# Mixture-of-experts stage of a fused Flamingo block: tiles fixed per expert, split weights kept, rows scattered to the output

## The reference

```python
x = x + tanh(g_xattn[0]) * L0_attention(layernorm(x), ctx)      # 32 heads, 8 KV heads
x = x + tanh(g_ffn[0])   * L0_blockdiagonal_ffn(layernorm(x))
x = x + tanh(g_xattn[1]) * L1_group_attention(layernorm(x), ctx)  # "x3" after this line
xf = layernorm(x).reshape(1024, 512)
selected = argmax(softmax(xf @ gate_w.T + gate_b))              # one of 8 experts per token
y[n] = xf[n] @ expert_w[selected[n]].T + expert_b[selected[n]]
x = x + tanh(g_ffn[1]) * y
```

## Time and profile before

| | us |
|---|---|
| median of 3 runs (840.06 to 843.03) | 842.01 |
| the profiled execution | 839.19 |
| its span, first to last instruction | 837.4 |
| busy in the span: PE / DVE / ACT / POOL | 767.1 / 484.6 / 490.6 / 344.4 |
| mean granted TensorE clock, as a share of full speed | 0.959 |

### The profile page before, as it was taken

How to read it: one execution, slowest core, us unless ns; L and a number is a source line. 1 busy time by engine, 2 the same in 40 slices (tenths; PEclk the granted TensorE clock), 3 DMA queues, 4 the chain that set the end, 5 groups by cost and what they waited for, 6 DMA issues and landing times. The chain is left out here.

```text
span 837.4 us, 13956 instructions
## 1 busy us (share of the span) xinstructions
PE 767.1 (92%) x3914; PEld 604.0 (72%) x3914; DVE 484.6 (58%) x889; ACT 490.6 (59%) x1836; POOL 344.4 (41%) x647
## 2 busy tenths in 40 slices
PE   5999988999999999999999999999999795778990
PEld 3888867888888887888887888888876242445760
DVE  4775304565655655556565655655666467646773
ACT  5543237667676675766766676676663566324760
POOL 0330024453443543444353453443322467135884
PEclk9999989999999999999999999999999799867995
DMA  9545631021021021012012003000200659513436
GB/s 306 183 122 154 188 102 64 14 76 64 13 77 63 14 76 64 13 50 88 13 32 94 25 13 113 25 13 14 101 2 10 204 179 411 196 76 117 146 127 213
DMA packets 46216, 80.68 MB, mean 96 GB/s; under 512 B 5192, under 2 KB 25672, under 8 KB 42704
## 3 DMA queue, kind: packets, MB, share of 16 engines
q1 hardware_dynamic: 43536, 71.66, 25.1%
q0 software_dynamic: 2624, 8.39, 3.0%
HBM read 55.40 MB, written 24.64 MB: 96 GB/s over the span
## 5 line engine op out<-in xcount | busy, mean ns | idle before, releaser
L557 ACT ACTIVATE p_sb<-p_sb,nmax 128x128 f32<-128x128 f32 x256 | 99.7, 391 | 132.5 <-DVE nmax L721 132.5
L649 POOL TENSOR_TENSOR v_lo<-v_raw,v_hi 128x128 fp32r<-128x128 f32 x64 | 29.7, 464 | 259.0 <-ACT v_hi L595 259.0
L744 DVE TENSOR_TENSOR pT_lo<-banks,pT_hi 128x512 fp32r<-128x512 f32 x64 | 44.3, 692 | 49.9 <-ACT pT_hi L570 49.9
L786 PEld LDWEIGHTS banks<-kT,qT_sb 128*128 128x128 f32 x512 | 67.4, 192 | 7.2 <-ACT qT_sb L565 1.8
L786 PE MATMUL banks<-kT,qT_sb 128*128 128x128 f32 x512 | 68.2, 277 | 1.4 <-ACT qT_sb L565 1.4
L654 POOL TENSOR_TENSOR p_sb<-p_sb,rsum 128x512 f32<-128x512 f32 x64 | 66.7, 1041 | 5.6 <-DVE rsum L740 5.6
L602 ACT ACTIVATE q_junk<-banks 128x128 f32<-128x128 f32 x256 | 66.2, 272 | 3.4 <-PE banks L798 3.4
L712 DVE TENSOR_TENSOR oT_lo<-banks,oT_hi 128x512 fp32r<-128x512 f32 x64 | 44.1, 689 | 36.2 <-ACT oT_hi L552 36.1
L393 PE MATMUL banks<-w_hi,ctx_hi 128*128 128x512 f32 x128 | 53.8, 420 | 8.7 <-DVE ctx_lo L324 8.6
L750 DVE SCALAR_TENSOR_TENSOR x_sb<-banks,tgates,x_sb 128x512 f32<-128x512 f32 x64 | 48.1, 751 | 19.2 <-PE banks L828 19.2
L552 ACT ACTIVATE oT_hi<-banks 128x512 fp32r<-128x512 f32 x64 | 38.1, 595 | 35.5 <-PE banks L839 31.4
(11 more groups left out here) (262 smaller groups left out, 2174.0 us busy)
## 6 DMA issues: line engine op xcount, KB each, us to landing
w_raw<-in_wq_l SPq DMA_DIRECT2D x8, 1024.0 KB, 5.6
w_raw<-in_wo_l SPq DMA_DIRECT2D x8, 1024.0 KB, 4.8
exp_w<-in_exp_w_l SPq DMA_DIRECT2D x8, 1024.0 KB, 13.5
kT_scr<-kT_st SPq DMA_DIRECT2D x16, 256.0 KB, 2.3
v_scr<-v_st SPq DMA_DIRECT2D x16, 256.0 KB, 2.3
sorted_x<-ctx_nat SPq DMA_DIRECT2D x1, 3840.0 KB, 11.9
hid<-sorted_x SPq DMA_DIRECT2D x15, 256.0 KB, 2.7
sorted_y<-ctx_nat SPq DMA_DIRECT2D x15, 256.0 KB, 2.0
```

Source lines behind the costliest of these rows:

```text
L557: last = act.activation(p_sb[:, b % 2, h * P:(h + 1) * P], p_sb[:, b % 2, h * P:(h + 1) * P], ACT.Exp, bias=nmax[:, b % 2, h:h + 1], accum ...
L786: last = pe.matmul(s_ps[:, h * P:(h + 1) * P], qT_sb[:, b % 2, h * P:(h + 1) * P], kT[:, b * P:(b + 1) * P], start=True, stop=True)
```

## The change

- The end of the block and the barrier between `middle` and `experts` are gone; both stages share one block. POOL clears the semaphores of `attention` inside `middle`, behind its fourth scatter. `keep_clock` is gone.
- The raw rows of x3 are scattered, with reciprocal root, shift and token number in 4 more columns (`ROW` = 516), to a region of 1024 rows per expert. A position no longer depends on the counts of the other experts, so the work is done in two halves of 4 blocks (`choose`, `position`, `scatter`). ACT normalises a row tile after it is loaded.
- The gate weights are centred (each column's mean subtracted) so that logits can be taken from raw rows; they are multiplied by the reciprocal root afterwards.
- Tiles 0 to 7 are the first 128 rows of each expert in a fixed `ORDER`; tiles 8 to 14 are found at run time (`list_tiles`). The weights are split once for each expert and kept, in 128 KB of each partition. DVE makes `lo` parts 0 to 2, POOL part 3 (of the first expert POOL makes all). Tiles 8 to 14 split no weights; PE and POOL read the expert number by `value_load`.
- POOL scales all biases by `tanh(g_ffn[1])` once and adds the expert's bias to the raw rows of each tile. DVE adds the product. POOL stores each tile by an indirect DMA straight to the output; rows that hold no token are out of bounds and are skipped. `sorted_y`, the gather and the last pass are gone.
- The regions are filled from one constant row during `attention` (8 DMAs of 2.1 MB). The gate's constants are loaded there too. The expert weights are loaded in the order 6, 7, then (after `y_done`) 4, 5, 0, 1, 2, 3, then the biases (2 MB).
- The tile loop is unrolled. Rows are loaded into 6 buffers, results have 3 banks.

```diff
@@ attention, SP @@
                 kT_half(1)
+                fill(g)
+            def fill(e):
+                sp.dma_start(d.sorted_x[e].rearrange("(k p) n -> p k n", p=P),
+                             s.empty[:, :].unsqueeze(1).to_broadcast([P, B, ROW])).then_inc(s.filled, 16)
...
+            fill(0)
             loads(1)
@@ middle @@
             for jt in range(KT):
                 scatter(0, jt)
+            nc.clear_and_free_semaphores(s.stage_sems)
+            pool.memset(s.recycled_flag[:, :], 0.0).then_inc(s.recycled, 1)
             scale_ctx(range(2))
...
+            for kt in range(KT):
+                pe.matmul(sm_ps[:, 320:320 + E], s.ones[:, :], s.gate_w[:, kt, :], start=(kt == 0), stop=(kt == KT - 1))
             pe.matmul(sm_ps[:, 0:B], s.group_mean[:, :], s.zmv[:, :, 0], start=True, stop=True).then_inc(gmean_done, 1)
@@ middle, SP @@
-            for e in (0, 1, 2, 3, 6, 7):
-                sp.dma_start(s.exp_w[:, e, :, :], d.exp_w[e]).then_inc(s.exp_ld, 16)
+            for e in (6, 7):
+                sp.dma_start(s.exp_w[:, e, :, :], d.exp_w[e]).then_inc(s.exp_ld[e // 2], 16)
             sp.wait_ge(y_done, B)
-            for e in (4, 5):
-                sp.dma_start(s.exp_w[:, e, :, :], d.exp_w[e]).then_inc(s.exp_ld, 16)
+            for e in (4, 5, 0, 1, 2, 3):
+                sp.dma_start(s.exp_w[:, e, :, :], d.exp_w[e]).then_inc(s.exp_ld[e // 2], 16)
+            sp.wait_ge(res_done, B)
+            sp.dma_start(s.exp_b[:, :, :], d.exp_b).then_inc(s.exp_b_ld, 16)
@@ experts, SP @@
+            sp.wait_ge(scattered, 16 * B)
+            for t in range(TILES):
+                slot = t % SLOTS
+                if t >= SLOTS:
+                    sp.wait_ge(stored[slot], 16 * (t // SLOTS))
...
+                sp.dma_start(xs[:, slot, :], rows).then_inc(xs_ld[slot], 16)
@@ experts, ACT @@
+            for b in BY_POOL:
+                act.activation(s.z[:, b, :], s.z[:, b, :], ACT.Identity, scale=s.a_col[:, b:b + 1]).then_inc(scaled_z, 1)
+            split_w(0)
+            copy_x3T(0)
...
+            copy_x3T(3)
+            seed(0)
...
+            seed(1)
+            split_w(1)
+            run([(split_x, 1), (normalise, 2), (split_next_w, 2)])
@@ experts, POOL @@
+            split_w(0, (0, 1))
+            rstd(0)
+            split_w(0, (2, 3))
+            rstd(1)
...
+            scatter(0)
+            pool.wait_ge(s.exp_b_ld, 16)
+            scatter(1)
+            pool.tensor_scalar(s.exp_b[:, :, :], s.exp_b[:, :, :], s.tgates[:, 3:4], None, ALU.mult).then_inc(bias_scaled, 1)
+            def add_bias(t):
...
+                pool.tensor_tensor(xs[:, slot, 0:D], xs[:, slot, 0:D], s.exp_b[:, e, :], ALU.add).then_inc(biased, 1)
+            def store(t):
+                pool.wait_ge(res_done, t + 1)
+                pool.indirect_dma_start(out=d.out_rows, in_=xs[:, slot, 0:D], in_offset=None,
+                                        out_offset=IndirectOffsetOnAxis(ap=xs[:, slot, TOKEN:TOKEN + 1].bitcast(I32), axis=0),
+                                        bounds_check=T - 1, oob_is_err=False).then_inc(stored[slot], 16)
+            run([(split_next_w, 1), (add_bias, 0), (store, -1)])
@@ experts, DVE @@
...
+            choose(0)
...
+            half_var(1)
+            position(0)
+            shift(1)
+            choose(1)
+            position(1)
+            run([(split_x, 1), (add_y, -1), (split_next_w, 1)])
@@ experts, PE @@
+            for b in range(B):
+                transpose_x3(b)
+                if b:
+                    gates(b - 1)
+            gates(B - 1)
...
+            ranks(0)
+            ranks(1)
...
+            run([(transpose_tile, 1), (multiply, 0)])
```

More of the change, by code:

```diff
@@ L42 @@
 EPS = 1e-5
[L43 to L46, removed]
+EXTRA = B - 1
+TILES = E + EXTRA
+ROW = D + 4
+RSTD, SHIFT, TOKEN = D, D + 1, D + 2
+ORDER = (6, 7, 4, 5, 0, 1, 2, 3)
+SLOTS = 6
+NOWHERE = 1e9
+GATE_LOADS = 8
+ARENA, SIDE = 144 * 1024, 28 * 1024
 QTOK = 2 * P
@@ L1304, in experts @@
         logit, top = m.sb("logit", [P, B, E]), m.sb("top", [P, B])
         cand, first = m.sb("cand", [P, B, E]), m.sb("first", [P, B])
[L1306 to L1309, removed]
+        hot, hot_sum = m.sb("hot", [P, B, E]), m.sb("hot_sum", [P, 2, E])
@@ L1372, in experts @@
-        stage = ExitStack()
-        block = stage.enter_context(nc.Block())
+        fuller, tiles = m.sb("fuller", [P, E, EXTRA]), m.sb("tiles", [P, E])
+        below, end = m.sb("below", [P, E, E]), m.sb("end", [P, E])
+        past, begin = m.sb("past", [P, EXTRA, E]), m.sb("begin", [P, EXTRA])
+        tile_e, tile_row = m.sb("tile_e", [P, EXTRA]), m.sb("tile_row", [P, EXTRA])
+        tile_i, row_i = m.sb("tile_i", [P, EXTRA], I32), m.sb("row_i", [P, EXTRA], I32)
+        x3T = s.xn
+        xs, xn, xsT_hi, xsT_lo = s.xs, s.xn, s.xsT_hi, s.xsT_lo
@@ new lines, in experts, with static_expert, run @@
+        BY_POOL = (4, 5)
+        LO_POOL = (3,)
+        LO_DVE = tuple(kt for kt in range(KT) if kt not in LO_POOL)
+        def static_expert(t):
+            return ORDER[t] if t < E else None
+        def run(stages):
+            last = max(-ahead for _, ahead in stages)
+            first = max(ahead for _, ahead in stages)
+            for i in range(-first, TILES + last):
+                for stage, ahead in stages:
+                    if 0 <= i + ahead < TILES:
+                        stage(i + ahead)
@@ L1401, in _ @@
+            for i in range(SLOTS):
+                sp.wait_ge(stored[i], 16 * len(range(i, TILES, SLOTS)))
         @block.scalar
@@ L1581, in split_x, with update, stats @@
-            def split_x(t, slot, r):
+            over = lambda ap, n=HB: ap.unsqueeze(1).to_broadcast([P, n, E])
+            def update(b):
+                dve.wait_ge(s.res_done, b + 1)
+                dve.scalar_tensor_tensor(out=xrow[:, b, 0:D], in0=s.z[:, b, :], scalar=s.a_col[:, b:b + 1],
+                                         in1=s.x[:, b, :], op0=ALU.mult, op1=ALU.add).then_inc(x3_done, 1)
+            def stats(b):
+                if b in BY_POOL:
+                    dve.wait_ge(x3_pool, BY_POOL.index(b) + 1)
+                else:
+                    dve.wait_ge(x3_done, b + 1 - sum(q < b for q in BY_POOL))
+                dve.bn_stats(s.bn[:, b, :], xrow[:, b, 0:D]).then_inc(bn_done, 1)
@@ new lines, in _ @@
+            dve.wait_ge(s.a_done, 1)
+            dve.wait_ge(s.centred, B)
+            update(0)
+            update(1)
+            stats(0)
+            update(2)
+            stats(1)
+            aggregate(0)
+            update(3)
+            stats(2)
+            aggregate(1)
+            stats(3)
+            aggregate(2)
+            aggregate(3)
+            half_var(0)
+            stats(4)
+            update(6)
+            aggregate(4)
+            stats(5)
+            shift(0)
@@ new lines, in gates @@
+            def gates(b):
+                pe.wait_ge(x3T_copied, b + 1)
+                for kt in range(KT):
+                    last = pe.matmul(logit_ps[b // HB][:, b % HB * E:(b % HB + 1) * E], x3T[:, b % 2, kt * P:(kt + 1) * P],
+                                     s.gate_c[:, kt, :], start=(kt == 0), stop=(kt == KT - 1))
+                last.then_inc(logit_done, 1)
+            pe.wait_ge(s.recycled, 1)
+            pe.wait_ge(s.gate_centred, 1)
+            pe.wait_ge(s.row_done, B)
```

608 lines of the change are left out of this document (288 added, 320 removed).

## The result

The changed kernel takes 846.61 us (median of 6 runs, 842.44 to 849.72) beside 841.84 for the kernel before: a ratio of 1.0055, 95% interval 1.0031 to 1.0080. In a second set of runs it was 841.25 beside 839.35, 1.0023 (1.0003 to 1.0043). The forecast was 826.0, with a range of 813 to 837 and a chance of 0.05 for slower. It was wrong.

A forecast was written before the change was run, and what follows sets the result against it. The prediction took a chain of waits as the bound: front 49.8 us, loop 54.6, tail 20.9. Terms -16.6 - 2.4 + 1.0 + 1.9 = -16.1 took the span from 837.4 to 821.3, the median to 826.0; range 813 to 837.

The forecast's parts named there:

- The tail: From the last matmul to the end: 4.3 us instead of 20.9, saving 16.6 us.
- The front: From `a_col` to the first product: gates from 716.5 at the lower clock, first product at 759.5, saving 2.4 us.
- Rival one: The front runs at the full clock, 2.4 GHz: 10 us more off, 816 us; chance 0.22.
- The drain in the middle: POOL's semaphore clearing in `middle` brings a drain that delays the scatters there: 1.0 us taken, up to 2.4.
- Rival two: POOL's indirect store in the tile loop takes 2.5 us to issue: 14 us more, 840 us; chance 0.12.
- The loop: Tile loop: POOL bounds tiles up to 7 at 4.3 us each; 1.9 us longer overall, from 3.5 shorter to 6 longer.
- The scaling of the biases: On POOL between the last scatter and the first product: 6.2 us, hidden, costing nothing.
- The last seven tiles: End of the tile loop, no weight splits: PE sets the pace at 3.3 us a tile, 1.8 us less in all.
- What hides the rest: Fills in SP's queue during attention: 6.5 us each, with 21.5 us until the load behind is used, so no cost.
- Rival three: Fills in SP's queue hold up attention's loads, from 18 us a fill; at 26 us, 48 us more, 874; chance 0.05.

The follow-up runs named there:

- e11: Changed kernel with fills half a group earlier, bias scaling and splits moved, attention's loop written out, seven idle matmuls ahead of the gates: 806.65 us, ratio 0.9603 to before.
- e8_one_column: Changed kernel with POOL's bias add cut to one of its 512 columns: 829.84 us, ratio 0.9877 to the kernel before.
- e1: Changed kernel with each 2 MB fill issued half a group earlier: 832.3 us, ratio 0.9930 to the kernel before.
- e6: Changed kernel with fills half a group earlier, bias scaling on ACT, tile list and most weight splits ahead of the first tile: 819.31 us, ratio 0.9761 to before.
- e3: Changed kernel with the bias scaling on ACT as eight instructions, not one on POOL: 837.82 us, ratio 0.9992 to the kernel before.
- e4: e3 with the tile list and most weight splits moved ahead of the tile loop, none on POOL from tile 1 on: 833.41 us, ratio 0.9947 to before.

## Why the prediction was wrong, by its own steps

*The tail: right.* It gave 4.3 us from the last product to the end; it is 5.4, and 15.5 us were saved of 16.6.

*The front: right, on the careful side.* Gates were to begin at 716.5 on before's time scale, with the clock at 0.50 throughout; they began at 732.81, which less the 16.6 us by which `a_col` is later in the first profile is 716.2, and the clock was 0.50 in every window of 4 us from 728 to 776. First product: 45.7 us after `a_col`, against 47.4 forecast and 49.9 before. Rival one, the front at full clock, did not happen, and `e11` shows that even a warmed clock does not outlast the gates.

*The drain in the middle: nothing* in the second profile, 1.0 forecast.

*Rival two, a dear store:* it did not happen. POOL's store took 1.90 us for the first tile, 1.26 where DVE's splits are beside it and 0.98 in the last seven, where 1.9 was the point from which it would decide.

*The loop, "POOL is the new bound, at 4.3": this step failed.* Tiles 2 to 7 took 29.0 us (first products at 787.46 and, of tile 8, at 816.45), 4.8 each, and tile 0 alone 8.5 (774.27 to 782.77). What bound them was neither POOL nor DVE alone but both by turns. I added up each engine's busy time, DVE 3.3 us, POOL 4.3, and took the longer sum. Where two engines need one port, what they do with it has to be added: DVE's splits 1.9 and POOL's split and addition 2.6 make 4.5, and DVE's other 1.4 lie beside that only where the order allows. That is an estimate. What the trace shows is that of the seven groups of three splits four took 1.88 us and three were held, for 3.4, 3.8 and 2.5 us (the table under `e8_one_column`). The clue was there, two POOL operations of 3.05 us beside DVE's, where they take 2.5 alone; I booked it as POOL being slower and did not ask what DVE lost. The scaling of the biases, "costs nothing" at 6.2 us, took 10.65 and reached into the loop, where it and POOL's next four operations held DVE's cast. The term came to +8.5 to +10 instead of +1.9. The last seven tiles ran at 3.2, as forecast.

*"What hides the rest", the fills at nothing: this step failed, and it was the larger one.* I asked which data stands behind a fill in SP's queue and found 21.5 us of slack, which is true: ACT never waited for a DMA at the line that was L578. What stood behind it was not data. At a branch back, ACT's instructions come through the same DMA engines, and the fill was issued 6 us ahead of it. The price is 12.8 us by the run that adds nothing else. Rival three named the place and the right victim, attention, by another mechanism and with a threshold of 18 us a fill, which the fills, at 8.8 us each and not 6.5, stayed well under; so its chance of 0.05 was no cover. In the trace of before both halves could be seen: ACT's 2.12 us of "issue" at 315.96, just at the branch, and SP's burst of loads beside it. I had not looked for idle time inside attention, since the change put no instruction there.

The Trainium skill, "Runtime: NRT & Kernel Launch", section "Instruction fetch mechanics", says that a taken branch whose target is not in the pages at hand forces a fetch of the target's page by DMA before the engine can go on. The runs agree, with 2.1 us at a quiet moment; that the wait grows to 5.9 to 6.3 us behind a fill and two loads is what they add.

With the terms at their measured size, the sum is -15.5 - 4.2 + 12 + 9 = +1.3 us; the two medians are +4.8 and +1.9. What is left of the first, 3.5 us, stays open; the two intervals overlap, and how often the stall in the middle comes was not followed further.

## What to carry to other kernels

A large transfer put into a quiet stretch is not free because the next load has slack: look where the engines' loops branch back, and keep the DMA engines empty there, or write the loop out. When work is shared out between DVE and POOL, first mark every operation of DVE that has two SBUF inputs or copies within SBUF; count the large ones and POOL's as one queue, so put their sum, not the longer of the two, against PE. And take two profiles before a stall is blamed on the change.

## What the runs showed of the hardware that I had not expected

- A branch back costs ACT 2.0 to 2.1 us with little traffic in the kernel before (2.5 to 2.8 in `e1` and `e6`) and 5.9 to 6.3 with a 2 MB fill and two 1 MB loads under way; straight code shows no stall beside the same traffic. PE's clock falls to 0.50 behind the longer stall at the first branch.
- A DVE cast of 7 columns, 0.16 us alone, took 5.60, until the last of five POOL operations without a gap was over. Without the scaling beside it in `e3` it took 0.16. Three small operations with two SBUF inputs, just ahead of it, were held for 0.25 us or not at all. POOL pays too: its indirect DMA took 1.90 us instead of 0.97 where it met a group of three splits (785.90, beside the group at 785.00), and in `e4` up to 1.50.
- POOL's one scaling of 128x4096 took 10.65 us; ACT did the same in 4.99, as eight instructions of 128x512.
- With PE busy for 4.00 of 4.00 us with short matmuls in each window from 736 to 752, the granted clock stayed at 0.50 in the changed kernel's front. In `e11` it fell from 1.00 to 0.50 during the same work.
